# A Mamba, cross-attention and experts decoder layer: stationary w1 and w3 in the expert products, and one 96-column product for the step size's low rank and the rows of B and C

## The reference, cut to what matters

```python
# 1. Mamba
xr = x @ W_in                                  # 128 -> 2 x 256
u = silu(causal_conv4(xr[..., :256]) + conv_b)
x_dbl = u @ W_x                                # 256 -> 64 + 16 + 16
delta = softplus(x_dbl[..., :64] @ W_dt + b_dt)
Bm, Cm = x_dbl[..., 64:80], x_dbl[..., 80:96]
hs = scan(exp(delta[..., None] * A), delta[..., None] * Bm[:, :, None, :] * u[..., None])
y = einsum('bldn,bln->bld', hs, Cm) + u * D
x = layernorm(x + (y * silu(xr[..., 256:])) @ W_out)
# 2. causal cross-attention with 16 heads of 8 and rotary positions on ctx, second layer norm
# 3. experts: each token goes to the two best of 8
for e in range(8):
    h = silu(x @ w1[e].T) * (x @ w3[e].T)      # 128 -> 512
    out += wte[:, e:e + 1] * (h @ w2[e].T)     # 512 -> 128
```

## Time and profile before

| | |
|---|---|
| median of 3 runs | 1072.79 us (1070.91 to 1076.31) |
| the profiled execution's own time | 1072.76 us |
| its span | 1071.0 us |
| busy TensorE, its weight loads | 944.1 us (88%), 537.3 us |
| busy VectorE, ScalarE, GpSimd | 683.6, 716.7, 567.9 us |
| expert loop on TensorE | 803.37 to 1030.77 |
| first scan | starts 50.74 |

### The profile page before, as it was taken

How to read it: one execution, slowest core, us unless ns; L and a number is a source line. 1 busy time by engine, 2 the same in 40 slices (tenths; PEclk the granted TensorE clock), 3 DMA queues, 4 the chain that set the end, 5 groups by cost and what they waited for, 6 DMA issues and landing times.

```text
span 1071.0 us, 28079 instructions
## 1 busy us (share of the span) xinstructions
PE 944.1 (88%) x9703; PEld 537.3 (50%) x9704; DVE 683.6 (64%) x1379; ACT 716.7 (67%) x2212; POOL 567.9 (53%) x387
## 2 busy tenths in 40 slices
PE   6699999989899899998989879878739999999997
PEld 2344554454454455445545435543416666666662
DVE  1377787786777678677777867867535444444437
ACT  2577886986897788588779847756604444444446
POOL 2487368459729937954972984592232323223310
PEclk9899999999999999999999979988959999999999
DMA  4515105200700610340060051004221111111135
GB/s 120 123 38 139 31 2 110 62 12 28 143 14 21 138 31 18 78 98 10 16 149 12 20 116 27 12 12 158 97 63 35 40 44 40 44 40 44 40 110 156
DMA packets 69227, 66.69 MB, mean 62 GB/s; under 512 B 9728, under 2 KB 63104, under 8 KB 68736
## 3 DMA queue, kind: packets, MB, share of 16 engines
q1 hardware_dynamic: 63856, 55.59, 21.1%
q0 software_dynamic: 4352, 8.99, 2.3%
q10 hardware_dynamic: 912, 0.67, 0.3%
HBM read 49.09 MB, written 16.13 MB: 61 GB/s over the span
## 4 chain that ended last, share of the span: by engine, by line
PE 48%; issue 19%; POOL 13%; ACT 10%; DVE 9%; DMA 2%; SPq 0%; POOLq 0%; DVEq 0%; ACTq 0%
PE pair_a L1687 6%; PE pair_b L1688 6%; PE bank L1701 6%; ACT prob L695 6%; POOL xg L530 4%; POOL prob L498 4%; PE y_ps L1408 3%; PE y_ps L1693 3%; PE pair_b L1488 3%; PE bank L1305 2%; PE y_ps L1488 2%; PE bank L1499 2%; POOL hst L498 2%; DVE hst L924 2%; DVE prob L924 2%
## 5 line engine op out<-in xcount | busy, mean ns | idle before, releaser
L654 ACT ACTIVATE decays<-w,a_neg 128x256 f32<-128x256 f32 x512 | 220.5, 510 | 31.0 <-DVE hst L924 17.5
L569 POOL DMA_INDIRECT y<-aoT,dest x72 | 69.4, 963 | 173.9 <-DVE aoT L1235 169.6
L498 POOL TENSOR_TENSOR hst<-hst,c_rep 128x1024 f32<-128x1024 f32 x64 | 151.2, 2367 | 15.3 <-DVE hst L924 14.4
L498 POOL TENSOR_TENSOR prob<-prob,c_rep 128x1024 f32<-128x1024 f32 x56 | 132.2, 2365 | 7.3 <-DVE prob L924 6.5
L530 POOL DMA_INDIRECT xg<-x_all,pos x64 | 64.6, 1009 | 91.7 <-DVE pos L1074 80.5
L1194 DVE TENSOR_TENSOR zpos<-zabs,pair_b 128x512 f32<-128x512 f32 x74 | 51.0, 689 | 81.4 <-PE pair_b L1688 81.4
L924 DVE TENSOR_TENSOR_SCAN prob<-decays,pair_b 128x1024 f32<-128x1024 f32 x32 | 73.1, 2284 | 44.8 <-issue 29.3
L695 ACT ACTIVATE prob<-pair_b,nmax 128x128 f32<-128x128 f32 x256 | 90.2, 400 | 4.8 <-DVE nmax L982 4.8
L695 ACT ACTIVATE prob<-y_ps,nmax 128x128 f32<-128x128 f32 x256 | 90.6, 413 | 0.0
L1408 PE MATMUL y_ps<-hst,sum 128*32 128x256 f32 x512 | 69.8, 420 | 19.3 <-POOL prob L498 19.3
L490 POOL TENSOR_TENSOR w<-diag,b_tok 128x1024 f32<-128x1024 f32 x32 | 60.6, 1924 | 48.1 <-ACT b_tok L636 26.0
(11 more groups left out here) (287 smaller groups left out, 2157.7 us busy)
## 6 DMA issues: line engine op xcount, KB each, us to landing
w<-d_dram SPq DMA_DIRECT2D x64, 256.0 KB, 6.6
c_rep<-c_dram SPq DMA_DIRECT2D x64, 128.0 KB, 4.0
qk<-xg SPq DMA_DIRECT2D x79, 65.0 KB, 1.9
d_dram<-zpos SPq DMA_DIRECT2D x8, 512.0 KB, 3.2
xn<-in_x SPq DMA_DIRECT2D x8, 256.0 KB, 3.0
cn<-in_ctx SPq DMA_DIRECT2D x8, 256.0 KB, 3.2
mask_b<-in_mask SPq DMA_DIRECT2D x8, 256.0 KB, 3.1
w<-in_w1T SPq DMA_DIRECT2D x1, 2048.0 KB, 7.7
```

What stands on the lines that cost most here:

```text
L498: g_.tensor_tensor(by_state(ring(k)), by_state(ring(k)), c_rep[:, :, toks[r]].rearrange("p q (i t) -> p i q t", i=2), ALU.mult).then_inc(s ...
L569: pool.indirect_dma_start(y2[:, :], bass.IndirectOffsetOnAxis(ap=dest[:, b:b + 1], axis=0), ys[:, b % 4, :], None).then_inc(s[f"y_out{b % ...
L654: last = A(by_state(decays[:, k % 2, :])[:, :, q, :], delta_rep[:, b, toks[r]].rearrange("p (i t) -> p i t", i=2), ACT.Exp, scale=a_neg[:, ...
```

## The change

Experts: `up` now takes the w1 and w3 of the tile's expert as the weights, in four pieces of 128 columns each, and moves the 128 columns of xsT through them. The result has the hidden features on the partitions, so that `down` takes it as it is: `gated_t`, the copy to `gT` and their semaphores go. The w1 of a tile is copied by ScalarE (`hold_w1`), the w3 by VectorE (`hold_w3`), out of the tile of all experts into a fixed tile `w13`, two buffers deep, four tiles ahead of `down`. The results of `down` alternate between banks 5 and 6, VectorE copies them ahead of its gate, and TensorE waits for the gate of two tiles before in `up`.

Step size: W_x is one tile of 96 columns, `low_steps` makes the low rank and the rows of B and C with one product per half of u, and `c_rows` goes. ScalarE copies rows 64 to 95, permuted, in two instructions right behind `dtl_out`, both copies lie side by side in `dtl`, and `step` waits for both. `b_columns` moves to k = 6, `btok_out` to k = 7, `ln_scale2` behind the copies. There are 8 early weight loads instead of 11.

The diff, cut to its core:

```diff
-        w_dt = sb("w_dt", [P, P])
+        w_x = sb("w_x", [P, 2, DTR + 2 * NST])
+        w_dt = sb("w_dt", [P, DIN])
         b_dt = sb("b_dt", [P, 2])
         w_out = sb("w_out", [P, 2, D])
         a_log = sb("a_log", [P, NQ, NB])
@@ -98,7 +97,7 @@
         rotk = sb("rotk", [P, 2, T])
...
-        c_copy = dtl[0:2 * NST, :]
+        c_copy = dtl[DTR:DTR + 2 * NST, :]
...
-        gT = decays[:, 0, :].rearrange("p (b c n) -> p b c n", b=2, c=FC)
+
+        w13 = u
...
-        for r in range(2):
-            load(w_dtl[:, :, r, :], a["W_x"][:, :, 0:DTR])
-        load(w_bc[:, :, :], a["W_x"][:, :, DTR:DTR + 2 * NST])
-        for h in range(2):
-            load(w_dt[h * DTR:(h + 1) * DTR, :], a["W_dt"][:, h * P:(h + 1) * P])
+        load(w_x[:, :, :], a["W_x"])
+        load(w_dt[0:DTR, :], a["W_dt"])
...
+            sp.wait_ge(s["up_ps"], 1 + 2 * (NT + 2))
+            sp.wait_ge(s["w1_sb"], NT + 4)
+            sp.wait_ge(s["w3_sb"], NT + 4)
...
-                A(dtl[:, :], bank[b], ACT.Copy).then_inc(s["dtl_sb"], 1)
+                A(dtl[0:DTR, :], bank[b][0:DTR, :], ACT.Copy).then_inc(s["dtl_sb"], 1)
...
-                at(act, "z_ps", 2 * m + 2)
-                at(act, "c_ps", m + 1)
-                A(c_copy, bank[b][0:2 * NST, :], ACT.Copy).then_inc(s["c_sb"], 1)
+                at(act, "dtl_ps", m + 1)
+                for r in range(2):
+                    last = A(c_copy[:, toks[r]].rearrange("p (y i t) -> p y i t", y=2, i=2), by_halves(bank[b][DTR:DTR + 2 * NST, :])[:, r], ACT.Copy)
+                last.then_inc(s["c_sb"], 1)
...
+            c_out(0, 1)
...
-            c_out(0, 0)
...
-                        if k == 2:
-                            ln_scale2(w)
...
                         if k == 2:
                             dtl_out(e, 5)
+                            c_out(e, 5)
+                    if w is not None and k == 2:
+                        ln_scale2(w)
...
                             step_log(e)
                         if k == 7:
-                            c_out(e, 7)
-                        if k == 10:
                             btok_out(e, 7)
...
+            def hold_w1(j, b):
+                e = act.value_load(table[0:1, 0, bass.ds(j, 1)], min_val=0, max_val=E - 1)
+                A(w13[:, b, 0, :], w1[:, bass.ds(e, 1), :].rearrange("p a f -> p (a f)"), ACT.Copy).then_inc(s["w1_sb"], 1)
+
+            act.wait_ge(s["table_sb"], 1)
+            act.wait_ge(s["w13_load"], 32)
+            hold_w1(0, 0)
+            hold_w1(1, 1)
...
             x_out(2, 0)
+            hold_w1(2, 0)
             silu(1, 1)
+            hold_w1(3, 1)
             with act.Fori(0, NT // 2) as it:
                 for b in range(2):
                     j = it * 2 + b
-                    act.wait_ge(s["gT_ps"], j + 1)
-                    A(gT[:, b], bank[4 + b].rearrange("p (c n) -> p c n", c=FC), ACT.Copy).then_inc(s["gT_sb"], 1)
                     x_out(j + 3, 1 - b)
                     silu(j + 2, b)
+                    hold_w1(j + 4, b)
...
-            early(dve, "gate_sb y_sb")
+            early(dve, "gate_sb y_sb y_sb")
...
+            def hold_w3(j, b):
+                e = dve.value_load(table[0:1, 0, bass.ds(j, 1)], min_val=0, max_val=E - 1)
+                v_.tensor_copy(w13[:, b, 1, :], w3[:, bass.ds(e, 1), :].rearrange("p a f -> p (a f)")).then_inc(s["w3_sb"], 1)
+
...
-                    gate(j + 2, b % 2)
                     dve.wait_ge(s["y_ps_s"], j + 1)
                     if not (isinstance(it, int) and b < 4):
                         dve.wait_ge(s[f"y_out{b % 4}"], (2 * it + b // 4) * 16)
-                    v_.tensor_copy(ys[:, b % 4, :], bank[6][:, b % 2 * P:(b % 2 + 1) * P]).then_inc(s["y_sb"], 1)
+                    v_.tensor_copy(ys[:, b % 4, :], bank[5 + b % 2][:, 0:P]).then_inc(s["y_sb"], 1)
+                    gate(j + 2, b % 2)
+                    hold_w3(j + 4, b % 2)
                     destinations(j + 3, (b + 3) % 4, 2 * it + (b + 3) // 4, (b + 3) % 8)
...
+            dve.wait_ge(s["table_sb"], 1)
+            dve.wait_ge(s["w13_load"], 32)
+            hold_w3(0, 0)
+            hold_w3(1, 1)
             for j in range(3):
                 destinations(j, j, 0, j)
             gate(0, 0)
+            hold_w3(2, 0)
             gate(1, 1)
+            hold_w3(3, 1)
...
             def low_steps(m, b):
+
                 at(pe, "u_sb", 2 * m + 2)
                 if m:
                     at(pe, "h_sb", NU * (m - 1) + 1)
                 for h in range(2):
-                    last = MM(bank[b], w_dtl[:, h].rearrange("p r n -> p (r n)"), u[:, m % 2, h, :], start=(h == 0), stop=(h == 1))
+                    last = MM(bank[b][0:DTR + 2 * NST, :], w_x[:, h, :], u[:, m % 2, h, :], start=(h == 0), stop=(h == 1))
                 last.then_inc(s["dtl_ps"], 1)
 
             def step(m, h, b):
                 at(pe, "dtl_sb", m + 1)
+                at(pe, "c_sb", m + 1)
                 if m and not h:
                     at(pe, "h_sb", NU * (m - 1) + 1)
-                r = slice(DTR * h, DTR * h + DTR)
-                MM(bank[b], w_dt[r, :], dtl[r, :], start=True, stop=True).then_inc(s["z_ps"], 1)
-
-            def c_rows(m, b):
-                at(pe, "u_sb", 2 * m + 2)
+                MM(bank[b], w_dt[0:DTR, h * P:(h + 1) * P], dtl[0:DTR, :], start=True, stop=True).then_inc(s["z_ps"], 1)
+
+            def b_columns(m, b):
+
+                at(pe, "c_sb", m + 1)
                 if m:
                     at(pe, "lg_sb", m - 1)
                 if m == 1:
                     at(pe, "duT_sb", 2)
-                for r in range(2):
-                    for h in range(2):
-                        last = MM(bank[b][0:2 * NST, toks[r]], w_bc[:, h, :], by_halves(u[:, m % 2, h])[:, r], start=(h == 0), stop=(h == 1))
-                last.then_inc(s["c_ps"], 1)
-
-            def b_columns(m, b):
-
-                at(pe, "c_sb", m + 1)
-                at(pe, "v_sb", m)
                 for t in range(S):
-                    last = TR(bank[b][:, t * 2 * NST:(t + 1) * 2 * NST], c_copy[:, t * P:(t + 1) * P], ident[0:2 * NST, 0:2 * NST])
+                    last = TR(bank[b][:, t * 2 * NST:(t + 1) * 2 * NST], c_copy[:, t * P:(t + 1) * P], ident[DTR:DTR + 2 * NST, DTR:DTR + 2 * NST])
...
-                at(pe, "c_sb", min(g + 2, G))
+                at(pe, "btok_sb", min(g + 2, G))
...
-            c_rows(0, 0)
...
-                            c_rows(e, 7)
+                            b_columns(e, 7)
...
-                    if k == 9 and e is not None:
-                        b_columns(e, 7)
...
-            def up(j, b):
-                e = pe.value_load(table[0:1, 0, bass.ds(j, 1)], min_val=0, max_val=E - 1)
+            def up(j, b, again=False):
+
+                if again:
+                    pe.wait_ge(s["gate_sb"], j)
                 pe.wait_ge(s["xsT_sb"], j + 1)
-                MM(bank[b], xsT[:, b, :], w1[:, bass.ds(e, 1), :].rearrange("p a f -> p (a f)"), start=True, stop=True).then_inc(s["up_ps"], 1)
-                MM(bank[2 + b], xsT[:, b, :], w3[:, bass.ds(e, 1), :].rearrange("p a f -> p (a f)"), start=True, stop=True).then_inc(s["up_ps"], 1)
-
-            def gated_t(j, b):
-                pe.wait_ge(s["gate_sb"], 1 + j + 1)
+                pe.wait_ge(s["w1_sb"], j + 1)
                 for c in range(FC):
-                    last = TR(bank[4 + b][:, c * P:(c + 1) * P], gg[:, b, c * P:(c + 1) * P], ident[:, :])
-                last.then_inc(s["gT_ps"], 1)
+                    last = MM(bank[b][:, c * P:(c + 1) * P], w13[:, b, 0, c * P:(c + 1) * P], xsT[:, b, :], start=True, stop=True)
+                last.then_inc(s["up_ps"], 1)
+                pe.wait_ge(s["w3_sb"], j + 1)
+                for c in range(FC):
+                    last = MM(bank[2 + b][:, c * P:(c + 1) * P], w13[:, b, 1, c * P:(c + 1) * P], xsT[:, b, :], start=True, stop=True)
+                last.then_inc(s["up_ps"], 1)
 
             def down(j, b):
                 e = pe.value_load(table[0:1, 0, bass.ds(j, 1)], min_val=0, max_val=E - 1)
-                pe.wait_ge(s["gT_sb"], j + 1)
+                pe.wait_ge(s["gate_sb"], 1 + j + 1)
                 pe.wait_ge(s["y_sb"], 1 + j)
                 for c in range(FC):
-                    last = MM(bank[6][:, b * P:(b + 1) * P], gT[:, b, c, :], w2[:, bass.ds(e, 1), c, :].rearrange("p a d -> p (a d)"),
+                    last = MM(bank[5 + b][:, 0:P], gg[:, b, c * P:(c + 1) * P], w2[:, bass.ds(e, 1), c, :].rearrange("p a d -> p (a d)"),
...
             rows_t(0, 0, 0, 0)
...
             with pe.Fori(0, NT // 4) as it:
...
-                    gated_t(j + 1, 1 - b % 2)
+                    up(j + 2, b % 2, True)
                     down(j, b % 2)
```

14 lines of the change are left out of this document (5 added, 9 removed).

## The result

The changed kernel takes 1038.76 us (median of 4 runs, 1037.55 to 1039.02) against 1072.23 before (4 runs, 1070.91 to 1076.31): a ratio of 0.9695, with a 95% interval of 0.9679 to 0.971. The forecast was 1037, the range 1027 to 1048. The total is close because misses of opposite sign nearly cancel: the front and the later groups gained some 5 us less than forecast, group 1 and the start of the expert stage nearly 4 more. The parts are what is worth reading.

A forecast was written before the change was run, and what follows sets the result against it. TensorE was taken to bound the experts, GpSimd the groups from the third on. Experts 27.0, front 5.0 and first two groups 3.7 sum to 35.7 off 1072.76: 1037 us, own range 1031 to 1043, with rivals 1 and 2 1027 to 1048.

The forecast's parts named there:

- The experts, 26.6: In the 72 expert tiles, TensorE sets the pace and a tile falls from 3.16 to 2.79 us, gaining 26.6.
- rival 3: In the expert tiles, weight loads pace TensorE at 0.121 us a record: tile 3.01, total 1052.9; 7 in 100.
- 5: In the expert tiles, the new weight loads in `up` stand open: tile 4.72 us, total 1176.0; 2 in 100.
- Rival 4: In the expert tiles, VectorE becomes the bound, its w3 copy waiting for GpSimd's scatter: 2.99 us, total 1051.5; 4 in 100.
- The stage's start, 0.4: At the start of the expert stage, the transposes ahead of the loop go, giving 0.44 us once.
- The front, 5.0: Up to the first scan: it comes at 45.7 instead of 50.74, gaining 5.0 us (2.1 to 8.6).
- the step size is stored 2.1 earlier: In the front, the step size is stored at 34.6 instead of 36.73, with `c_rows` out of the chain.
- What is late next are the loads of delta: In the front, once the convolutions start 8.6 us earlier, the loads of delta hold the first scan.
- Groups 1 and 2, 1.84 each: In the two groups without scatters, TensorE reaches later scans 1.84 us earlier: 3.7 in all (0 to 3.7).
- Groups 3 to 7, nothing: In these groups GpSimd's queue is full, so nothing is gained (from 3.3 us lost to 9.2 gained).
- Rival 1: The front and first groups give nothing, held by loads or GpSimd; only the experts gain: 1045.8 us; 15 in 100.
- Rival 2: Every group gains its 1.84 us, as a shorter TensorE queue moves more than GpSimd: 1027.9; 9 in 100.

The follow-up runs named there:

- e6: The changed kernel with a second, unread copy of w3 ahead of each real one in VectorE's queue: 1042.09 us, one time.
- e3: The changed kernel with GpSimd's first diagonals held until VectorE's two products delta * u are done: 1036.59 us, ratio 0.9665.
- e1: The kernel before with only the experts changed, step size and rows of B and C as before: 1045.22 us, ratio 0.9742.
- e2: The kernel before with only the step size changed (one product of 96 columns), experts as before: 1067.17 us, ratio 0.9942.
- e4: The changed kernel with the residual's product moved ahead of the sums over the states in TensorE's queue at the 14th state: 1040.09 us, ratio 0.969.
- e9: The kernel before with GpSimd's first diagonals held until VectorE's two products delta * u are done: 1071.24 us, ratio 0.9995.

## Why the prediction was right, and where it was not

- **The experts, 26.6.** Right, in size and mechanism. Four products of 128 columns in 0.89 and the transpose in 0.11 make 2.79; TensorE never waits for w1, w3 or the gate; the four transposes and the wide products are gone. The weight loads lie under the products, though all use all rows: rivals 3 (tile 3.01) and 5 (4.72) fall. With 5 falls, for this case, the sentence of the Trainium skill (TensorE: Matmul & The Clock Gate, Part 3, "The mechanism") that was cited for it. The same section also lets a load be pulled ahead when it targets the background weight buffer, which the forecast left out; the 2.79 agrees with that, and no row names the buffer. The 0.121 of rival 3 was a misreading: 0.97 holds the whole last load of 0.19, and (0.97 - 0.19) / 7 = 0.111 is the distance of the loads. Rival 4 falls by e6. VectorE's 1.76 a tile and ScalarE's 1.52 (109.37 / 72) are a little below the 1.85 and 1.59 taken.
- **The stage's start, 0.4.** It gained 2.80 in the pair of profiles and 1.3 by the means of the others (8.64 and 8.54 with the old experts; 7.48, 7.39, 7.20, 7.25 and 7.17 with the new). The step counted only the four transposes ahead of the loop, 0.44. Another 0.7 is the gap ahead of the first products, where the table read stood, which the forecast costed at nothing. The rest, 1.6 in the pair and about 0.1 by the means of the others, goes with the clock, which was back at 1.00 in after 3.7 us from the first transpose, the earliest of the traces without products ahead of the rows, and in before after 7.8.
- **The front, 5.0.** The failed step is "the step size is stored 2.1 earlier": it was stored 0.2 later (0.5 earlier by the means of the traces in which the diagonals are not held, 37.0 against 37.5), because the move of `b_tok`'s copy started GpSimd's diagonals ahead of VectorE's products, which took 4.58 (e3: 1.29 without them). The forecast followed the move of `c_out` through four queues, but not GpSimd's start behind `b_tok`. "What is late next are the loads of delta" was right. That the first scan came at 45.50 with the products undisturbed, next to the 45.7 forecast, is partly luck: delta was stored at 33.38, 1.2 earlier than the 34.6 of the forecast, and the loads and decays took 12.1 from there, 1.0 longer than its 11.1.
- **Groups 1 and 2, 1.84 each.** Right: 1.96 and 1.86 between e1 and e2; by the means of all traces, without e4 and the group 1 of before, 1.7 and 1.9. The 1.4 more of group 1 against before is a stretch at half rate in before's group 1, from 58.1 to 61.6: with it the group lasts 85.77, while e1 and e9, which have the same code there and not this stretch, show 84.18 and 83.63.
- **Groups 3 to 7, nothing.** Right for GpSimd's time: with the clock at 1.00 a group lasts 89.8 to 90.0 with `c_rows` and 89.8 to 90.1 without. Wrong for the clock: 1.84 less of TensorE lengthened its wait from 2.2 to 2.5, and one group in four more fell to the 1.2 GHz level, for 1.6. Nothing is what the forecast's queues give; the loss is outside them. By the forecast's own sign ("if a later group changes its length by over 1 us") this part was wrong.
- **Rivals 1 and 2.** Rival 1 (front and first groups nothing, 1045.8) falls: they gave 6.8 in the pair. Its number is that of e1, 1045.22, in which part 2 is left out. Rival 2 had every group gain 1.84; e4's groups, freed of the half rate, show that even then none does.
- **The range.** The low end of the forecast's own range, 1031, doesn't come out of its terms: 8.6 for 5.0 in the front gives 1033.5. The result lies far from it.

By chance the front's -3.2 and the clock's -1.9 met the +2.4 of the stage's start and the +1.3 of group 1. What stays open is why the half rate comes in two or three of four groups with the same wait, and why the loads of delta differ by 2 us between executions.

## What to carry to other kernels

When a copy is moved to where it is ready sooner, look at which engine it releases, and what that engine then runs beside: VectorE's two products beside GpSimd's diagonals cost 3.3 us here on the path, and one wait bought it back. Where another engine sets the pace, taking work off TensorE may cost time: waits of 2.1 to 2.6 us were followed by a stretch at 1.2 GHz in 24 of 36 groups here. A product that is needed anyway, moved into the wait, removed it in 12 of 12, and gained only where nothing else came to wait for it (e4 lost in groups 1 and 2 what it gained later). A duration that is read from a row with a neighbour beside it is a price for that company only.
